# Linear attention on one core: rounding gate, up and down weights beside the tiles, with magnitudes on ScalarE and the down weights turned three blocks at once

## The reference

```python
def _L0_attn_ref(x, Wq, Wk, Wv, Wo):
    q = (x @ Wq.T).reshape(Bx, Lx, NUM_HEADS, HEAD_DIM)      # 16 heads of 16
    ...
    q = jax.nn.elu(q) + 1.0
    k = jax.nn.elu(k) + 1.0
    kv = jnp.einsum('blhd,blhe->blhde', k, v)
    kv_cumsum = jnp.cumsum(kv, axis=1)
    k_cumsum = jnp.cumsum(k, axis=1)
    out = jnp.einsum('blhd,blhde->blhe', q, kv_cumsum)
    denom = jnp.clip(jnp.einsum('blhd,blhd->blh', q, k_cumsum), 1e-06, None)
    ...

def fp4_quant_dequant(x):                                    # blocks of 16 along the last dim
    scale = jnp.max(jnp.abs(xb), axis=-1, keepdims=True) / 6.0
    scale = jnp.maximum(scale, jnp.float32(1e-12))
    xn = xb / scale
    idx = jnp.searchsorted(_MID, jnp.abs(xn))
    q = _GRID[idx] * jnp.sign(xn) * scale
    ...
x = x + 0.5 * _L0_ffn_ref(_layernorm(x), ...)
x = x + _L0_attn_ref(_layernorm(x), ...)
x = x + 0.5 * _L0_ffn_ref(_layernorm(x), ...)
x = x + 0.5 * _L1_ffn_ref(_layernorm(x), w_gate, w_up, w_down)   # rounds x, h and its weights
...
```

## Time and profile before

| what | value |
|---|---|
| median of 3 runs | 3241.82 us (3233.46 to 3247.18) |
| the profiled execution's own time | 3211.57 us |
| its span | 3209.6 us |
| mean granted TensorE clock | 0.972 |
| TensorE matmul busy | 3039.3 us, 95% |
| VectorE busy | 2457.1 us, 77% |
| ScalarE busy | 2058.9 us, 64% |
| GpSimd busy | 555.1 us, 17% |
| the linear attention stage | about 450 to 755 us of the span |

### The profile page before, as it was taken

The page is one execution under the profiler, slowest core; times in us unless marked ns, Lnnn a source line. Parts: engine busy times, 40 slices in busy tenths (PEclk is TensorE's granted clock), DMA queues, the critical chain, the costliest instruction groups (busy, mean ns, idle before and its releaser), DMA issues. The chain is left out here.

```text
span 3209.6 us, 62375 instructions
## 1 busy us (share of the span) xinstructions
PE 3039.3 (95%) x24516; PEld 2019.9 (63%) x24516; DVE 2457.1 (77%) x4826; ACT 2058.9 (64%) x3764; POOL 555.1 (17%) x612
## 2 busy tenths in 40 slices
PE   7999979987999979987999999999999999997998
PEld 6899968776989969984343333334333333343998
DVE  7533468875533389984988999999999999983987
ACT  5544534444644546652577888887888888876665
POOL 3322235543412242220000000000000000001222
PEclk9999989998999989997799999999999999998999
DMA  4211120002211110003303012020303030000000
GB/s 128 85 44 36 50 70 2 2 2 61 94 40 42 35 43 1 1 1 94 41 28 49 20 19 25 12 31 2 42 2 42 2 42 2 2 2 1 14 18 23
DMA packets 60962, 100.45 MB, mean 31 GB/s; under 512 B 7632, under 2 KB 44160, under 8 KB 57984
## 3 DMA queue, kind: packets, MB, share of 16 engines
q1 hardware_dynamic: 54144, 78.62, 11.3%
q0 software_dynamic: 6528, 17.83, 1.8%
HBM read 65.36 MB, written 30.93 MB: 30 GB/s over the span
## 5 line engine op out<-in xcount | busy, mean ns | idle before, releaser
L2258 DVE TENSOR_REDUCE smxp<-psum 128x1 f32<-128x512 f32 x2048 | 1258.6, 681 | 39.8 <-PE psum L2109 38.4
L2218 ACT ACTIVATE spr<-psum 128x512 f32<-128x512 f32 x2048 | 1113.9, 596 | 266.9 <-PE psum L2133 219.4
L2109 PE MATMUL psum<-sks,sqs 48*128 48x512 f32 x2048 | 783.3, 463 | 12.4 <-DMA sqs<-q_parts 11.6
L2133 PE MATMUL psum<-sqs,sks 50*128 50x512 f32 x2048 | 752.7, 452 | 0.0
L2150 PE MATMUL psum<-spr,sv 128*32 128x256 f32 x8192 | 657.0, 392 | 11.3 <-ACT sot L2225 8.7
L2109 PEld LDWEIGHTS psum<-sks,sqs 48*128 48x128 f32 x2048 | 322.0, 189 | 432.8 <-issue 382.4
L2150 PEld LDWEIGHTS psum<-spr,sv 128*32 128x32 f32 x8192 | 162.8, 108 | 380.9 <-ACT spr L2218 293.7
L2133 PEld LDWEIGHTS psum<-sqs,sks 50*128 50x128 f32 x2048 | 301.8, 185 | 16.0 <-issue 9.3
L1835 POOL MEMSET fhqb<- 128x64 f32 x3 | 0.3, 152 | 1498.4 <-POOLq L2022 1498.4
L526 PE MATMUL psum<-w_a,hsa_hi 128*128 128x256 f32 (+1 forms) x1088 | 198.3, 281 | 1.4 <-DVE hsa_lo L776 1.4
L526 PE MATMUL psum<-w_b,hsb_hi 128*128 128x256 f32 (+1 forms) x1088 | 197.1, 279 | 0.3 <-DVE hsb_lo L776 0.3
(11 more groups left out here) (413 smaller groups left out, 5942.1 us busy)
## 6 DMA issues: line engine op xcount, KB each, us to landing
sks<-q_parts SPq DMA_DIRECT2D x42, 256.0 KB, 9.1
sqs<-q_parts SPq DMA_DIRECT2D x42, 256.0 KB, 19.7
q_parts<-spart SPq DMA_DIRECT2D x16, 512.0 KB, 2.9
f_routed_a<-yoa SPq DMA_DIRECT2D x9, 512.0 KB, 2.9
f_routed_b<-yob SPq DMA_DIRECT2D x9, 512.0 KB, 2.9
x<-in_L_attn_x_dram SPq DMA_DIRECT2D x8, 512.0 KB, 7.2
yoa<-in_L_ffn_w_dram SPq DMA_DIRECT2D x16, 256.0 KB, 2.8
xga<-f_sorted_a SPq DMA_DIRECT2D x8, 512.0 KB, 3.8
```

Source lines behind the costliest of these rows:

```text
L2109: e.matmul(bank(what), QS[n % 2][rows, pr, q0:q0 + P], KS[n % 2][rows, pr, jc * GW:(jc + 1) * GW], start=True, stop=True, tile_position=(H ...
L2133: e.matmul(out, KS[n % 2][rows, pr, jt * P:(jt + 1) * P], QS[n % 2][rows, pr, ic * GW:(ic + 1) * GW], start=True, stop=True, tile_position ...
L2218: e.activation(PR[j % 2][:, HEAD[i], :], src, ACT.Exp, scale=float(DH) ** -0.5).then_inc(*done.up)
L2258: e.tensor_reduce(out[:, r // (2 * GT * IC), r // (2 * IC) % GT, r // 2 % IC, r % 2:r % 2 + 1], bank(what), AX.X, ALU.max).then_inc(*pm_fr ...
```

## The change

Weights are rounded with `QuantiseMax` in place of `Quantise`: VectorE does six steps (L156, L158, L160, then the scaled value at L223 with the sign turned, and two three-operand steps, L227 and L232), ScalarE computes the magnitude of the scaled value between them (L237), and GpSimd only multiplies (L240). The result is the same grid value.

VectorE's steps stand in different slots. Of chunk j, steps 0 to 3 are in pass 10+j as before; ScalarE's magnitude is at the end of its pass 10+j; steps 4 and 5 are in the first slot of pass 11+j, ahead of steps 0 to 3 of the next chunk; GpSimd's product is at the end of its pass 11+j; the turn is in pass 12+j as before. Two sets of scratch alternate, cut out of the same `qtmp`. Of the first down half: step 0 in pass 22, steps 1 to 3 in pass 23 with the magnitude at its end, step 4 in pass 24, step 5 in pass 25 with the product at its end, turned in both slots of pass 26. Of the second: 24, 26, 27, 28 and 29 in the same way. A down turn takes three blocks of 128 columns into the shared bank at once; ScalarE copies them with one instruction, or with two where the last block has 64 columns.

Two semaphores that `ffn1` had for itself are now shared with this stage (`row_scaled`, `row_magnitude`).

The excerpt gives, one below the other, the slots, then TensorE's, ScalarE's, VectorE's and GpSimd's part.

```diff
-                WS = 4 + 2 * CH + 3 + 2 * (C1 + 1)
-
-                def quantised_at(i):
-
-                    if 4 <= i < 4 + 2 * CH and i % 2 == 0:
-                        return (i - 4) // 2 // C1, (i - 4) // 2 % C1
-                    if i in (4 + 2 * CH, 5 + 2 * CH + C1):
-                        return 2, (0 if i == 4 + 2 * CH else 1)
-                    return None
+                DOWN = 4 + 2 * CH
+                DP = C1 // 2
+                WS = DOWN + 15
...
+                def quantise_w(j):
+
+                    if j < CH:
+                        a, c = divmod(j, C1)
+                        rows, nbk = rows_of(j), D // QB
+                        tmp = (qtmp[0][:, :, j % 2 * nbk:(j % 2 + 1) * nbk], qtmp[1][:, :, j % 2 * D:(j % 2 + 1) * D])
+                        q = QuantiseMax(gu[0:rows, a, c, :], D, rows, tmp, guq[j % 2][0:rows], wq_sum, wq_ok)
+                    else:
+                        q = QuantiseMax(dn[:, j - CH, :], H1, P, qtmp, dnq[:], wq_sum, wq_ok)
+                    return q.events(j, wq_y, wq_abs)
...
+                def vector_steps(i):
+
+                    if chunk_at(i, 5) is not None:
+                        return chunk_at(i, 5), (4, 5)
+                    if chunk_at(i, 4) is not None:
+                        return chunk_at(i, 4), (0, 1, 2, 3)
+                    return {DOWN: (CH, (0,)), DOWN + 1: (CH, (1, 2, 3)), DOWN + 3: (CH, (4,)), DOWN + 4: (CH + 1, (0,)),
+                            DOWN + 5: (CH, (5,)), DOWN + 7: (CH + 1, (1, 2, 3)), DOWN + 9: (CH + 1, (4,)),
+                            DOWN + 11: (CH + 1, (5,))}.get(i)
+
+                def magnitude_at(i):
+
+                    return CH if i == DOWN + 2 else CH + 1 if i == DOWN + 8 else chunk_at(i, 4)
+
+                def product_at(i):
+
+                    return CH if i == DOWN + 6 else CH + 1 if i == DOWN + 12 else chunk_at(i, 6)
...
-                    if 6 + 2 * CH <= i < 6 + 2 * CH + C1:
-                        return "down", 0, i - 6 - 2 * CH
-                    if 7 + 2 * CH + C1 <= i < 7 + 2 * CH + 2 * C1:
-                        return "down", 1, i - 7 - 2 * CH - C1
+                    if i in (DOWN + 7, DOWN + 8):
+                        return "down", 0, (i - DOWN - 7) * DP
+                    if i in (DOWN + 13, DOWN + 14):
+                        return "down", 1, (i - DOWN - 13) * DP
...
-                                e.transpose(misc[0:rows, 0:P], dnq[:, c * P:c * P + rows],
-                                            ident[:]).then_inc(*misc_in.up)
+                                for j in range(DP):
+                                    rows = rows_of(c + j)
+                                    m = e.transpose(misc[0:rows, j * P:(j + 1) * P],
+                                                    dnq[:, (c + j) * P:(c + j) * P + rows], ident[:])
+                                m.then_inc(*misc_in.up)
...
+                            if i is not None and magnitude_at(i) is not None:
+                                quantise_w(magnitude_at(i)).scalar(e)
...
-                                e.activation(wdT[0:rows, c, a * P:(a + 1) * P], misc[0:rows, 0:P],
-                                             ACT.Copy).then_inc(*misc_free.up)
+                                full = min(DP, C1 - 1 - c)
+                                m = e.activation(wdT[:, c:c + full, a * P:(a + 1) * P],
+                                                 misc[:, 0:full * P].rearrange("p (c n) -> p c n", n=P), ACT.Copy)
+                                if full < DP:
+                                    m = e.activation(wdT[0:R1, C1 - 1, a * P:(a + 1) * P],
+                                                     misc[0:R1, full * P:(full + 1) * P], ACT.Copy)
+                                m.then_inc(*misc_free.up)
...
-                            for step in range(7):
+                            if steps[0] == 1:
+                                e.wait_ge(*wq_ok(j))
+                            q = quantise_w(j)
+                            for step in steps:
+                                if step in (1, 5):
+                                    q.at = dv.now()
                                 q.vector(e, step)
...
+                            j = product_at(i)
+                            e.wait_ge(*wq_sum(j + 1))
+                            if 2 <= j < CH:
+                                e.wait_ge(*misc_in(misc_use["w", 7 + 2 * (j - 2)] + 1))
+                            if j == CH + 1:
+                                e.wait_ge(*misc_in(misc_use["w", DOWN + 8] + 1))
+                            quantise_w(j).gpsimd(e)
```

More of the change, by code:

```diff
@@ L1065, in attn0 @@
                 w_turn, w_hi, w_lo, wq_sum, wq_ok = (event(f"a0_{n}") for n in ("w_turn", "w_hi", "w_lo", "wq_sum", "wq"))
+                wq_y, wq_abs = event("row_scaled"), event("row_magnitude")
                 pool_ok, ones_ok = event("a0_masks"), event("a0_ones")
@@ L1075, in attn0, with rows_of, chunk_at @@
                 CH = 2 * C1
-                WS = 4 + 2 * CH + 3 + 2 * (C1 + 1)
-                def quantised_at(i):
-                    if 4 <= i < 4 + 2 * CH and i % 2 == 0:
-                        return (i - 4) // 2 // C1, (i - 4) // 2 % C1
-                    if i in (4 + 2 * CH, 5 + 2 * CH + C1):
-                        return 2, (0 if i == 4 + 2 * CH else 1)
-                    return None
+                DOWN = 4 + 2 * CH
+                DP = C1 // 2
+                WS = DOWN + 15
+                def rows_of(j):
+                    return P if j >= CH or j % C1 < C1 - 1 else R1
+                def quantise_w(j):
[7 more added lines that the diff above has]
+                    return q.events(j, wq_y, wq_abs)
+                def chunk_at(i, first):
+                    k, odd = divmod(i - first, 2)
+                    return k if 0 <= k < CH and not odd else None
+                def vector_steps(i):
[10 more added lines that the diff above has]
+                    return CH if i == DOWN + 6 else CH + 1 if i == DOWN + 12 else chunk_at(i, 6)
                 def turned_at(i):
@@ L1089, in turned_at @@
                         return "plain", i // 2, 0
-                    if 7 <= i < 7 + 2 * CH and i % 2:
-                        return "chunk", (i - 7) // 2 // C1, (i - 7) // 2 % C1
-                    if 6 + 2 * CH <= i < 6 + 2 * CH + C1:
-                        return "down", 0, i - 6 - 2 * CH
-                    if 7 + 2 * CH + C1 <= i < 7 + 2 * CH + 2 * C1:
-                        return "down", 1, i - 7 - 2 * CH - C1
+                    j = chunk_at(i, 7)
+                    if j is not None:
+                        return "chunk", j // C1, j % C1
+                    if i in (DOWN + 7, DOWN + 8):
+                        return "down", 0, (i - DOWN - 7) * DP
+                    if i in (DOWN + 13, DOWN + 14):
+                        return "down", 1, (i - DOWN - 13) * DP
                     return None
@@ L1395, in weights @@
                             i = weights_at(n, second)
[L1396 removed]
+                            if i is None or not vector_steps(i):
                                 return
[L1398 to L1409 removed]
+                            j, steps = vector_steps(i)
+                            if steps[0] == 0:
+                                if j < CH:
+                                    e.wait_ge(*gu_in[j // C1](2))
+                                else:
+                                    e.wait_ge(*dn_in(1))
+                                if 2 <= j < CH:
+                                    e.wait_ge(*wq_ok(j - 1))
+                            if steps[0] == 1:
[4 more added lines that the diff above has]
+                                    q.at = dv.now()
                                 q.vector(e, step)
@@ L1564, in _ @@
                             weights(n, True)
+                wq_y.close(CH + 2)
+                wq_abs.close(CH + 2)
                 for ev in (xn_ok, xhi, min_ok, exp_ok, v_ok, qk_ok, qkturn, qt_ok, st_ok, kv_ok, po_ok, os_ok, oturn,
@@ L1596, in ffn1 @@
                 hleft, hlo = event("f1_hleft"), event("f1_hlo")
-                xy, xabs, hy, habs = (event(f"f1_{n}") for n in ("xy", "xabs", "hy", "habs"))
+                xy, xabs, hy, habs = (event(n) for n in ("row_scaled", "row_magnitude", "f1_hy", "f1_habs"))
                 down_ok, u_ok, out_ok = event("f1_down"), event("f1_u"), event("x_out", 16)
```

28 lines of the change are left out of this document (3 added, 25 removed).

## The result

| | before | the change |
|---|---|---|
| median | 3238.6 us of 6 runs (3230.97 to 3247.43) | 3215.47 us of 6 runs (3205.15 to 3223.4) |
| ratio of the runs | | 0.9928, 95% interval 0.9904 to 0.9953 |
| span of the profiled execution | 3209.6 us | 3221.7 us |
| passes 11 to 21 of the linear attention | 93.33 us | 89.01 us |
| passes 22 to 29 | 85.25 us | 67.64 us |

The change is 23 us faster by the medians, 0.72% (0.47 to 0.96%). The profiled execution of the change is, with 3223.4 us, the longest of its six, and its span is even longer than that of before. So the gain must be read by stage and not from the two spans.

The account below looks back on a forecast made before the run. TensorE sets a floor of 7.91 us a pass in the linear attention, with VectorE's undivided down rounding the main excess. Gains of 17.0 (passes 22 to 29) and 4.2 (chunks) make 21.2, taken off 3241.82: 3221 us, range 3210 to 3234.

Parts of the forecast that it names:

- The down rounding: Passes 22 to 29: dividing the 7.4 us VectorE piece ends idle stretch and half clock; pass 22 becomes 8.1 us.
- The chunk passes: Passes 11 to 21: VectorE's slot falls from 2.40 to 2.08 us, passes to 8.10, 89.1 in all, gaining 4.2.
- the stalled step: Pass 11: L170 took 1.46 us, started 0.09 behind GpSimd's L1558 and ended when that did; pass 1.04 longer.
- The magnitudes: On ScalarE ahead of the copy L1356: twelve narrow ones cost nothing, the wide one 0.15 us in pass 24.
- Pass 26 and pass 29: Passes with triple down turns: 10.4 and 9.6 us, TensorE waiting for ScalarE's copies, idle about 2 us in pass 26.
- their 0.55: Passes 26 and 29: wider turns and copies, second copy and transposes add 0.55 us together, bounds 0.2 and 1.2.
- Nothing is charged: GpSimd loses its subtraction per chunk and multiplies after its pass's masks, over a microsecond before TensorE's turn: cost 0.
- Sum and total: Passes 22 to 29 gain 17.0 us, with the chunks 21.2; total 3221 us, timed median 30 above the profiled execution.
- A: Rival: one VectorE step per chunk pass loses to GpSimd, 1.04 us each for twelve; gain 9, 3233 us; chance 0.08.
- B: Rival: two lost races per chunk pass, 19.9 us, plus 6.2 on wide steps; 3247 us, slower; chance 0.03.
- C: Rival: ScalarE's magnitudes show, 0.42 us per narrow and 0.79 per wide, 6.6 together; 3227 us; chance 0.12.
- D: Rival: VectorE not the holder in plain chunk passes; pass 26 loses its clock (256-column matmuls 0.41); 3225 us; chance 0.12.

Follow-up runs that it names:

- The half alone: Only the down half of the change (divided rounding, triple turns), chunks as before, against the kernel before: ratio 0.9939, passes 10 to 31 185.31 us.
- the chunk half: Only the change's chunk steps, down weights rounded in one piece and turned singly, one pass later, against the kernel before: ratio 0.9977, passes 10 to 31 197.65 us.
- The run with the old arithmetic: The change's slots and triple turns with seven VectorE steps, no ScalarE magnitude, GpSimd's subtraction kept, against the change: passes 10 to 31 183.27 us, 180.85 in the change.
- the four single runs: Variants of the change on another chip: single down turns, old arithmetic, one more reduce, doubled magnitude; 3193.12, 3192.86, 3209.15, 3205.43 us.

## Why the prediction came out as it did

**The down rounding.** Right, in mechanism and size. Pass 22 was forecast at 8.1 and took 8.09; the idle stretch and the half clock are gone. The half alone, and the chunk half with the long passes back, show that it carries the gain. (The steps of a half stand in four VectorE places, not the five that the prediction counts; nothing was worked out from that number.)

**The chunk passes.** 8.10 was forecast, 8.09 measured in pass 16; eleven passes 89.01 against 89.1. The mechanism was right: VectorE was what held plain chunk passes, and 0.3 us off its slot brought them to where TensorE alone sets the pace. VectorE's slot is 2.06 us, forecast 2.08. But 8.10 was the middle between two bounds and not worked out; that it fits to 0.01 is luck. The reading of the stalled step was a little off, too: L170 did not end when GpSimd's L1558 did but 0.28 us behind it (525.08 against 524.80), just as L223 in the run with one reduce more.

**The magnitudes.** The narrow ones cost nothing that shows, and the doubled one shows how thin that is: 0.12 us in most passes, 0.33 in pass 10, and a lost race behind it. For the wide one pass 24 was charged 0.15; passes 23 and 24 together took 16.10, against 16.25 forecast. The cut between them moved, since L1538 came late once, and the next pass made it up.

**Pass 26 and pass 29.** Forecast 10.4 and 9.6, measured 10.19 and 9.52. The chain was the right one, the wait of L1232 for L1374. The sums were too high by 0.1 to 0.2; put down to the widths, their 0.55 was that much too large. TensorE idled 1.43 us in pass 26, 1.22 of them in one piece, not the 2 us forecast, and the clock stayed at 1.00.

**GpSimd.** "Nothing is charged" held for the change as it is. But the prediction did not say what the removed subtraction was worth in its new place. The run with the old arithmetic shows it: TensorE waited for up to 1.0 us in passes 26 and 29.

**Sum and total.** Forecast 21.2 us, 21.9 in passes 10 to 31 of the profile, 23.1 by the medians. The total confirms the size only roughly, since its interval runs from 15 to 31 us; it is the stage that tests the sum. That the profiled execution stood 30 us from the runs' median was left open, and remains so in part. A place for it can be seen in the profiles. The two MLP stages of layer 0 (up to the attention's first L126, and from the first L648 to `ffn1`'s first L223) take 450.7 and 422.5 us in the profile of before and 449.0 to 451.9 and 422.5 to 424.0 in the four single runs; in the five profiles taken among the timed runs they take 453.1 to 463.6 and 429.7 to 435.0. The single runs all have the change's new slots in them, so it isn't the change that lengthens these stages. Why they differ, and so why the kernel before took 3211.57 and 3214.77 us in single runs and 3238 in the timed ones, is not settled.

**The rivals.** A did not occur; its price, 1.04 a pass, was confirmed where it was forced: 9.47 in most passes against 8.41 in the one that escaped. B needs both races lost and was not seen. C did not occur: L1520 waited for L1400 once in passes 11 to 31, for 0.2 us. A whole second magnitude cost 0.12 in most passes, though near C's 0.42 in pass 10. Of D the first part, that VectorE was not the holder, is refuted by the x turn of pass 16, which followed close on L1506 before and no longer does, and by the three slot lengths with their three pass lengths. The second part is refuted by the clock of pass 26; the matmuls with 256 columns behind its idle took 0.28 to 0.29 us, but for the first (0.36), where 0.41 had been named as the sign.

## What to carry to other kernels

When a long piece of side work stands in one place of an engine's order, ask first what is queued behind it: here 7.4 us of VectorE in one pass cost 7 us and half clock behind it, and the same steps in slots of at most 1.8 us cost next to nothing there; what they did cost came from GpSimd, whose work for them ended too late for the turns. Price a slot by what the pass has left, and check the start of each VectorE step with two SBUF inputs against GpSimd's next instruction, since a few tenths of a microsecond decide over a whole one. Where the run-to-run spread is as large as the gain, compare the stretches of the stage that changed: here they repeated to 0.1 us while the two spans differed by 14.5.

## What was not expected of the hardware

A lost race cost nearly the same whatever brought it about. One reduce of 0.45 us ahead of L223 and one magnitude on another engine both made a pass about 1.0 us longer than the work itself explains (9.47 against 8.41 for pass 12 and pass 17 of the first, 8.99 for pass 11 of the second against 7.96 in the change), because L223 started 0.06 or 0.10 us behind GpSimd and ended some 0.3 behind the end of GpSimd's instruction.

The long piece was partly no work at all. In pass 22 of the kernel before, the wide steps L165 and L168 took this long, with GpSimd's instructions of that time below them:

```profile
617.41 1.48 DVE L165 TENSOR_SCALAR qw_y<-qw_y 128x704 int32<-128x704 int32 x1
618.92 1.47 DVE L168 TENSOR_SCALAR qw_y<-qw_y 128x704 f32<-128x704 f32 x1
...
617.02 1.48 POOL L1558 TENSOR_TENSOR aqe<-aqT,pair_mask 128x512 f32<-128x512 f32 x1 [2.90 <-ACT aqT L1379]
618.46 3.04 POOL L1536 TENSOR_TENSOR aat<-aat,causal 128x512 f32<-128x512 f32 x2
```

In the slots of the old-arithmetic run the same three wide steps, L170 among them, read:

```profile
624.68 0.52 DVE L165 TENSOR_SCALAR qw_y<-qw_y 128x704 int32<-128x704 int32 x1
...
632.60 0.52 DVE L168 TENSOR_SCALAR qw_y<-qw_y 128x704 f32<-128x704 f32 x1
633.15 0.89 DVE L170 TENSOR_TENSOR qw_y<-qw_y 128x704 f32<-128x704 f32 x1
```

With L170, 1.83 us in the earlier trace rows, the three took 4.78 us in pass 22 and take 1.93 in the slots. The other 2.85 were a hold-up: each of the three started while GpSimd was at work on the scores (617.02 to 621.50). In the slots GpSimd is idle while they run. Dividing the piece took that off VectorE, besides spreading the rest.
